# Score products of a small attention: four f32 products on all 128 rows, or twenty-four of the rounded type on 64 rows each

## The chip, the cores and the metric

The kernel runs on one core of one Trainium2 chip. Its time is the device time of one execution, in microseconds. TensorE multiplies, ScalarE and VectorE read its results from the accumulation banks and compute elementwise, SyncE (SP) and GpSimd (Pool) mostly start transfers.

## The reference, cut to what matters

A tower for 1024 samples. An encoder makes four "states" of width 512 per sample, each with a real and an imaginary part (`sr`, `si`). The stage of this case is the attention over the four states of one sample, with 8 heads of width 64:

```python
qr = heads(sr @ Wq_r.T + bq_r); qi = heads(si @ Wq_i.T + bq_i)   # k, v alike
ar = einsum('bhnd,bhmd->bhnm', qr, kr) + einsum('bhnd,bhmd->bhnm', qi, ki)
ai = einsum('bhnd,bhmd->bhnm', qi, kr) - einsum('bhnd,bhmd->bhnm', qr, ki)
w = softmax(sqrt(ar**2 + ai**2 + 1e-8) * HD**-0.5)
out_r = einsum('bhnm,bhmd->bhnd', w, vr); out_i = einsum('bhnm,bhmd->bhnd', w, vi)
attn_r = out_r @ Wo_r.T + bo_r; attn_i = out_i @ Wo_i.T + bo_i
```

Around it stand the encoders before (two large layers for each part, about the first half of the time) and, after it, a pairwise combination of the states and a small network.

## The kernel before

**Types.** The large products are done in three passes of a rounded type (`F32R`): each operand is split into a rounded part ("high") and the rest ("low"), and `split3` (lines 53 to 55) multiplies high x high, high x low and low x high into the same bank. The score products alone, with the turning and the mixing, are done on f32 operands directly.

**Blocks and steps.** `phase_states` takes 64 samples at a time: 16 blocks, each of 256 columns (`C`: 4 states x 64 samples), in two groups of 128 columns (`NG` = 2, each 32 samples with their 4 states). The width of 512 is done in 4 steps `m` of 128, that is two heads `h` of 64 each. `e` is 0 for the real and 1 for the imaginary part. Blocks 0, 1 and 15 are written out, 2 to 14 are a loop on every engine.

**TensorE's order.** In each step `m` of block `b`: `project(b, m, 0)` (Q: 24 products of 256 columns into bank `b_q`, there is only one) and `project(b, m, 1)` (K: 24 products, into one of two banks `b_k`); then, for the block before, `t_turn` (four transposes of the softmax weights, line 2014); then `score(b, m-1)` (line 2004); then `mix(b-1, m-1)` (weights times values, line 2025). After step 3 come `values(b, 0)` and `(b, 1)`, turn, score and mix of the last step, `values(b, 2)` and `(b, 3)`, and `project_out(b-1, m)` for the four `m`, 24 products each.

**Scores before.** The contraction is over both parts at once: `qs` holds, for one head, the real part of Q on partitions 0 to 63 and the imaginary part on 64 to 127. `ks` holds two arrangements of K next to each other, (real, imaginary) and (-imaginary, real), so that one product on 128 rows with 256 moving columns gives `ar` and `ai` of one head and one group. A step takes 2 heads x 2 groups = 4 such products.

**Who fills them.** ScalarE's `q_evac` adds the bias and copies Q from the bank into `qs` (4 operations on 64 partitions, line 1287). VectorE's `k_evac` makes the two arrangements of K (8 operations on 64 partitions, line 1590). `q_read` and `k_read` then free the banks and let `score` start. In the same step ScalarE also copies the turned weights (`pt_evac`, 1302), squares the scores (`t_square`, 1296) and rounds the attention's output (`o_high`, 1311, behind the mixing); VectorE spreads the weights over a mask (`spread`, 1639, behind the turns), takes the output's rest (`o_low`, 1648), and adds, masks and reduces the squared scores (`pick`, 1600 to 1609). The turns of the next step wait for `o_low`.

**Storing.** At a block's end, `t_high` (ScalarE, 1339) and `t_low` (VectorE, 1659) split the projected outputs of step `m` into slot `m % 2` of the tile `at`, and SP's `store_a` writes each step in four transfers of 128 KB. `t_high` of step `m` waits for the store of step `m - 2` (`a_stored`).

Of the kernel before, what the change touches and what calls it, by code (L numbers as in the profile page):

```python
# [14 lines left out]
P = 128  # L15
# [891 lines left out]
def phase_states(nc, g):  # L907
# [15 lines left out]
    with s.ctx:  # L923
# [8 lines left out]

        sx = sb_t("sx", [P, 2, 2, NG, KD, P], F32R)

        qs = sb_t("qs", [P, 2, 2, C])
        ks = sb_t("ks", [P, 2, 2, 2, C])
        v = sb_t("v", [P, NG, H, 2, HD])
        sq = sb_t("sq", [P, 2, W])
        m2 = sb_t("m2", [P, W])
# [1 line left out]
        ptl = sb_t("ptl", [P, 2, W])  # L941
        ohi = sb_t("ohi", [P, KD, 2, C], F32R)
        olo = sb_t("olo", [P, KD, 2, C], F32R)
        at = sb_t("at", [P, 2, 2, 2, C], F32R)
        thi, tlo = at[:, 0], at[:, 1]
        mg2 = sb_t("mg2", [P, KD, GH, N])
        tmag = sb_t("mag", [P, KD, GH, N])
        top = sb_t("top", [P, KD, GH])
# [45 lines left out]
        x_loaded = [s.sem(f"t_s_loaded{e}") for e in range(2)]  # L994
        projected = s.sem("t_projected")
        q_read = s.sem("t_q_read")
        k_read = [s.sem(f"t_k_read{h}") for h in range(2)]
        v_full = s.sem("t_v_full")
        v_read = s.sem("t_v_read")
        scored = s.sem("t_scored")  # L1000
# [82 lines left out]
        b_pm = g.ps[:, 5, :]  # L1083
        b_vo = g.ps[:, 6:8, :]
        b_val = [b_vo[:, 0, :], b_vo[:, 1, :], b_q, b_k[:, 0, :]]
        K_PARTS = ((0, 0, 0, 1), (0, 1, 1, 1), (1, 0, 1, 1), (1, 1, 0, -1))

        def half(h):
            return slice(h * HD, (h + 1) * HD)
# [166 lines left out]
        @block.gpsimd  # L1256
        def _(pool):
            def fold(t):
                pool.wait_ge(folded, t * 2 + 1)
                if not isinstance(t, int) or t < LAST:  # L1260
                    pool.wait_ge(newton, t * 2 + 3)
                pool.wait_ge(stored, t * 16)
                pool.tensor_tensor(sup[:, :, :], cs[:, :, 2, :], cs[:, :, 3, :], ALU.add).then_inc(folded, 1)

            pool.memset(k01[:, 0:1], FLOOR).then_inc(k_made, 1)
            pool.memset(k01[:, 1:2], 1.0).then_inc(k_made, 1)
            pool.wait_ge(ids_in, 16)
            for t in range(TT):
                pool.wait_ge(projected, (t + 2) * 8 + 5)
                for f, tbl in enumerate((g.tbl_0, g.tbl_1, g.tbl_2, g.tbl_3)):  # L1270
                    pool.indirect_dma_start(
                        out=emb[:, t, f * N:(f + 1) * N], out_offset=None, in_=tbl,
                        in_offset=bass.IndirectOffsetOnAxis(ap=ids[:, t, f:f + 1].bitcast(U32), axis=0)).then_inc(emb_in, 16)
            fold(0)
            with pool.Fori(1, LAST) as t:
                fold(t)
            fold(LAST)

        @block.scalar
        def _(act):  # L1280
            def q_evac(b, m):
                if not isinstance(b, int) or 4 * b + m >= 2:
                    act.wait_ge(scored, b * 8 + (2 * m - 2))
                act.wait_ge(projected, b * 8 + (2 * m + 1))
                for e in range(2):
                    for h in range(2):
                        ins = act.activation(qs[half(e), m % 2, h, :], b_q[half(h), e * C:(e + 1) * C], ACT.Identity,
                                             bias=bcol(M_Q + e, m, half(h)))
                    ins.then_inc(q_read, 1)

            def t_square(b, m):
                for h in range(2):
# [53 lines left out]

            def block_body(b, first):
                q_evac(b, 0)
                for m in range(1, KD):
                    q_evac(b, m)  # L1350
                    if not first:
                        pt_evac(b - 1, m - 1)
                    t_square(b, m - 1)
                    if not first:
                        o_high(b - 1, m - 1)
                    if first and m == 1:
                        pieces(M_V * KD, M_O * KD)
                    if first and m == 3:
                        pieces(M_O * KD, NP)
                if not first:  # L1360
                    pt_evac(b - 1, KD - 1)
                t_square(b, KD - 1)
                if not first:
                    o_high(b - 1, KD - 1)
                for i in range(4):
                    v_evac(b, i)
                t_magnitude(b)
                if not first and not last(b):
                    t_high(b - 1, 0)
                exponent(b)  # L1370
                if not first and not last(b):
                    for m in range(1, KD):
                        t_high(b - 1, m)

            blocks(act, block_body)
            block_body(LAST_B, False)

# [203 lines left out]

        @block.vector
        def _(dve):
            def k_evac(b, m):
                if not isinstance(b, int) or 4 * b + m >= 2:
                    dve.wait_ge(scored, b * 8 + (2 * m - 2))
                dve.wait_ge(projected, b * 8 + (2 * m + 2))
                for h in range(2):
                    for e, part, at_half, sign in K_PARTS:
                        ins = dve.tensor_scalar(ks[half(at_half), m % 2, h, part, :], b_k[half(h), m % 2, e * C:(e + 1) * C],  # L1590
                                                bcol(M_K + e, m, half(h)), float(sign), ALU.add, ALU.mult)
                    ins.then_inc(k_read[h], 1)

            def pick(b, m):

# [73 lines left out]
                                      ALU.subtract).then_inc(w_split, 1)  # L1669

            def block_body(b, first):
                k_evac(b, 0)
                for m in range(1, KD):
                    if not first:
                        spread(b - 1, m)
                    k_evac(b, m)
                    if not first:
                        o_low(b - 1, m - 1)
                    pick(b, m - 1)
                    if first and m == 1:  # L1680
                        pieces(M_V * KD, M_O * KD)
                    if first and m == 3:
                        pieces(M_O * KD, NP)
                pick(b, KD - 1)
                if not first:
                    o_low(b - 1, KD - 1)
                shift(b)
                if not first and not last(b):
                    t_low(b - 1, 0)
                total(b)  # L1690
                spread(b, 0)
                if not first and not last(b):
                    for m in range(1, KD):
                        t_low(b - 1, m)
# [259 lines left out]
        def _(pe):  # L1954
            def project(b, m, i):

                pe.wait_ge(w_split, (M_Q, M_K)[i] * KD + 2 * KD)
                if i == 0:
                    if not isinstance(b, int) or 4 * b + m >= 1:
                        pe.wait_ge(q_read, b * 8 + 2 * m)  # L1960
                elif not isinstance(b, int) or 4 * b + m >= 2:
                    for h in range(2):
                        pe.wait_ge(k_read[h], b * 4 + (m - 1))
                if m == 0 and not (isinstance(b, int) and b == 0):
                    pe.wait_ge(v_read, b * 4 - (1 - i))
                out = b_q if i == 0 else b_k[:, m % 2, :]
                for e in range(2):
                    pe.wait_ge(x_loaded[e], b * 32 + 32)
                    for k in range(KD):
                        w = ((M_Q, M_K)[i] + e) * KD + k  # L1970
                        mm = split3(pe.matmul, out[:, e * C:(e + 1) * C], whi[:, w, m * P:(m + 1) * P],
                                    wlo[:, w, m * P:(m + 1) * P], sx[:, e, 0, :, k, :], sx[:, e, 1, :, k, :],
                                    k == 0, k == KD - 1)
                mm.then_inc(projected, 1)

            def values(b, i):
                pe.wait_ge(w_split, M_O * KD)
                e, gr = i // 2, i % 2
                if i == 2:
                    pe.wait_ge(q_read, b * 8 + 8)  # L1980
                elif i == 3:
                    for h in range(2):
                        pe.wait_ge(k_read[h], b * 4 + 3)
                elif not isinstance(b, int) or b >= 2:
                    pe.wait_ge(t_split, b * 8 - (10 - 2 * i))
                elif b == 1:
# [5 lines left out]
                mm.then_inc(v_full, 1)  # L1992

            def score(b, m):
                pe.wait_ge(q_read, b * 8 + (2 * m + 2))
                for h in range(2):
                    pe.wait_ge(k_read[h], b * 4 + (m + 1))
                for h in range(2):
                    if not isinstance(b, int) or 4 * b + m >= 1:
                        pe.wait_ge(t_squared, b * 8 + (2 * m - 1 + h))  # L2000
                    for gr in range(NG):
                        cols = slice(gr * P, (gr + 1) * P)
                        out = b_sc[:, h, :].rearrange("p (a g c) -> p a g c", a=2, g=NG)[:, :, gr]
                        mm = pe.matmul(out, qs[:, m % 2, h, cols], ks[:, m % 2, h, :, cols], start=True, stop=True)
                    mm.then_inc(scored, 1)

            def t_turn(b, m):
                pe.wait_ge(pd_made, b * 4 + (m + 1))
# [219 lines left out]
def build(nc, g):  # L2228
    with ExitStack() as ctx:
# [10 lines left out]
        g.ids_sb = s.sb("ids", [P, TT, N], mybir.dt.int32)  # L2240
        g.emb = s.sb("emb", [P, TT, N * N])
        g.k01 = s.sb("k01", [P, 2])
        s.align(512)
        with ExitStack() as first:
            g.x_all = first.enter_context(nc.sbuf_tensor("x_all", [P, KI, TOK], F32))
# [102 lines left out]
```

## Time and profile before

| what | value |
|---|---|
| median of 3 runs | 2947.16 us (2946.24 to 2949.06) |
| the profiled execution | 2950.54 us |
| its span, first to last instruction | 2948.7 us |
| mean granted clock of TensorE | 0.979 |
| TensorE busy | 2815.6 us, 95% |
| VectorE busy | 2105.5 us, 71% |
| ScalarE busy | 1326.6 us, 45% |

The stage of the change lies from about 1424 to 2410 us; the first score product starts at 1437.7 us, the last at 2320.7 us. Records of TensorE overlap: each lasts longer than the distance to the next one's start, since products are pipelined. The distance between starts is what one costs in a dense stretch.

### The profile page before, as it was taken

The page shows a single profiled execution, that of the slowest core. Times are in us where ns is not written, and L with a number is a line of the kernel's source. Part 1 is how long each engine was busy: PE and PEld are TensorE (multiplying, and loading weights), DVE is VectorE, ACT ScalarE, POOL GpSimd, SP SyncE. Part 2 cuts the span into 40 slices and gives each one's busy share as a digit, 9 for nine tenths or more (in the row PEclk, how much of TensorE's full clock was granted, in tenths as well). Part 3 has the DMA queues.
Part 4 walks back from the last instruction along what each step waited for, and adds up shares of the span by engine and source line. Part 5 has one row for each costly group of instructions (what it writes and reads, how often), then busy time and mean ns, then how long its engine had stood idle before and what let it go on. Part 6 is the DMA issues. An engine that isn't in the chain of part 4 may idle for free. (4 is left out here: it accounts for less than half of the span.)

```text
span 2948.7 us, 40983 instructions
## 1 busy us (share of the span) xinstructions
PE 2815.6 (95%) x15040; PEld 2438.5 (83%) x15040; DVE 2105.5 (71%) x3170; ACT 1326.6 (45%) x2000; POOL 139.8 (5%) x177
## 2 busy tenths in 40 slices
PE   8999999998999989999699999999999899999797
PEld 6888888886788877888599999999999877777686
DVE  5788768763668856787667667766776759999863
ACT  2222432243534344333455555555555654555553
POOL 1000100001001010000001001000000000000000
PEclk9999999998999999999899999999999999999899
DMA  6565465545738776486422232233223464344310
GB/s 241 188 208 187 170 225 189 187 138 179 244 113 263 251 254 202 142 266 242 172 58 58 79 92 57 59 91 78 57 71 94 105 163 103 93 101 123 111 40 11
DMA packets 493712, 420.36 MB, mean 143 GB/s; under 512 B 282272, under 2 KB 397088, under 8 KB 493344
## 3 DMA queue, kind: packets, MB, share of 16 engines
q1 hardware_dynamic: 459168, 341.20, 38.2%
q0 software_dynamic: 17792, 60.89, 5.4%
q10 hardware_dynamic: 16640, 16.78, 1.7%
q8 instruction: 70, 1.15, 0.2%
q14 instruction: 42, 0.34, 0.0%
HBM read 328.62 MB, written 90.18 MB: 142 GB/s over the span
## 5 line engine op out<-in xcount | busy, mean ns | idle before, releaser
L53 PE MATMUL banks<-a_hi 128*128 128x512 f32 x1024 | 399.6, 390 | 14.3 <-DVE a_lo L353 14.3
L54 PE MATMUL banks<-a_lo,a_hi 128*128 128x512 f32 x1024 | 399.3, 390 | 0.0
L55 PE MATMUL banks<-a_hi,a_lo 128*128 128x512 f32 x1024 | 399.3, 390 | 0.0
L53 PE MATMUL banks<-b_hi 128*128 128x512 f32 x896 | 357.0, 398 | 24.3 <-DVE b_lo L760 14.0
L55 PE MATMUL banks<-b_hi,b_lo 128*128 128x512 f32 x896 | 352.5, 393 | 0.0
L54 PE MATMUL banks<-b_lo,b_hi 128*128 128x512 f32 x896 | 352.4, 393 | 0.0
L53 PE MATMUL banks<-t_sx,g_hi 128*128 128x256 f32 x1024 | 294.6, 288 | 26.5 <-DMA t_sx<-s_scr 26.5
L54 PE MATMUL banks<-t_sx,g_hi 128*128 128x256 f32 x1024 | 291.5, 285 | 0.0
L55 PE MATMUL banks<-t_sx,g_lo 128*128 128x256 f32 x1024 | 291.5, 285 | 0.0
L1590 DVE TENSOR_SCALAR t_ks<-banks,cols 64x256 f32<-64x256 f32 x512 | 236.5, 482 | 75.2 <-PE banks L55 67.9
L53 PEld LDWEIGHTS banks<-a_hi 128*128 128x128 f32 x1024 | 192.9, 188 | 54.6 <-DVE a_lo L353 14.7
L55 PEld LDWEIGHTS banks<-a_hi,a_lo 128*128 128x128 f32 x1024 | 192.8, 188 | 40.2
L54 PEld LDWEIGHTS banks<-a_lo,a_hi 128*128 128x128 f32 x1024 | 192.8, 188 | 40.0
L53 PEld LDWEIGHTS banks<-b_hi 128*128 128x128 f32 x896 | 170.4, 190 | 66.0 <-DVE b_lo L760 28.8
L53 PE MATMUL banks<-g_hi,s_axng 128*128 128x512 f32 x512 | 203.6, 398 | 18.2 <-DVE s_cs L1732 14.6
L53 PEld LDWEIGHTS banks<-t_sx,g_hi 128*128 128x128 f32 x1024 | 198.4, 194 | 27.2 <-issue 23.1
L54 PE MATMUL banks<-g_lo,s_axng 128*128 128x512 f32 x512 | 202.5, 395 | 0.0
L55 PE MATMUL banks<-g_hi,s_axng 128*128 128x512 f32 x512 | 202.3, 395 | 0.0
L55 PEld LDWEIGHTS banks<-b_hi,b_lo 128*128 128x128 f32 x896 | 170.4, 190 | 36.4
L54 PEld LDWEIGHTS banks<-b_lo,b_hi 128*128 128x128 f32 x896 | 170.8, 191 | 34.3
L54 PEld LDWEIGHTS banks<-t_sx,g_hi 128*128 128x128 f32 x1024 | 198.5, 194 | 0.1
L55 PEld LDWEIGHTS banks<-t_sx,g_lo 128*128 128x128 f32 x1024 | 198.3, 194 | 0.0
(192 smaller groups left out, 5828.9 us busy)
## 6 DMA issues: line engine op xcount, KB each, us to landing
w_ring<-w_first SPq DMA_DIRECT2D x192, 512.0 KB, 4.3
w_ring<-w_second SPq DMA_DIRECT2D x160, 512.0 KB, 5.0
t_sx<-s_scr SPq DMA_DIRECT2D x64, 512.0 KB, 4.3
a_scr<-t_at SPq DMA_DIRECT2D x256, 128.0 KB, 1.9
s_axng<-a_scr SPq DMA_DIRECT2D x64, 512.0 KB, 5.4
g_wraw<-w_pieces SPq DMA_DIRECT2D x74, 256.0 KB, 4.7
x_raw<-h_scr ACTq DMA_DIRECT2D x16, 1024.0 KB, 7.0
w_ring<-w_second SPq DMA_DIRECT2D x64, 256.0 KB, 5.0
```

Of the source, the lines that this page charges most:

```text
L53: mm(out, ahi, bhi, start=first, stop=False, **more)
L54: mm(out, ahi, blo, start=False, stop=False, **more)
L55: return mm(out, alo, bhi, start=False, stop=last, **more)
L1590: ins = dve.tensor_scalar(ks[half(at_half), m % 2, h, part, :], b_k[half(h), m % 2, e * C:(e + 1) * C], bcol(M_K + e, m, half(h)), float(s ...
```

## The change

Each score is now computed like the other large products, in three passes of high and low parts. `q_evac` makes the high part of Q for both heads at once (2 operations on 128 partitions) and a new `k_evac` on ScalarE the high part of K in three pieces: imaginary, real, minus imaginary (3 operations). VectorE's new `q_rest` and `k_rest` make the low parts (2 and 3 operations on 128 partitions) and free the banks. A head's 64 values of one part stand on 64 partitions, so a product contracts over 64 rows of the array: head 0 on the lower half, head 1 on the upper. Real and imaginary are two products that are added in the bank, times three passes: six products for each head and group, 24 in a step. For a group they are issued as six of head 0 and then six of head 1.

Two more things go with it. The tile `at` is dropped, and `thi`, `tlo` (what is stored) are now the high and low part of `qs`; so `q_evac` of steps 0 and 1 waits for the stores of the block before (`a_stored`). And `score` waits once for both heads' squares (`t_squared`) instead of once per head. The Pool queue computes the negated K bias `nbk` once at the stage's start.

```diff
@@ -932,8 +932,7 @@
 
         sx = sb_t("sx", [P, 2, 2, NG, KD, P], F32R)
 
-        qs = sb_t("qs", [P, 2, 2, C])
-        ks = sb_t("ks", [P, 2, 2, 2, C])
+        ks = sb_t("ks", [P, 2, 2, 3, C], F32R)
         v = sb_t("v", [P, NG, H, 2, HD])
         sq = sb_t("sq", [P, 2, W])
         m2 = sb_t("m2", [P, W])
@@ -941,8 +940,8 @@
         ptl = sb_t("ptl", [P, 2, W])
         ohi = sb_t("ohi", [P, KD, 2, C], F32R)
         olo = sb_t("olo", [P, KD, 2, C], F32R)
-        at = sb_t("at", [P, 2, 2, 2, C], F32R)
-        thi, tlo = at[:, 0], at[:, 1]
+        qs = sb_t("qs", [P, 2, 2, 2, C], F32R)
+        thi, tlo = qs[:, 0], qs[:, 1]
         mg2 = sb_t("mg2", [P, KD, GH, N])
         tmag = sb_t("mag", [P, KD, GH, N])
         top = sb_t("top", [P, KD, GH])
@@ -994,7 +993,9 @@
         x_loaded = [s.sem(f"t_s_loaded{e}") for e in range(2)]
         projected = s.sem("t_projected")
         q_read = s.sem("t_q_read")
-        k_read = [s.sem(f"t_k_read{h}") for h in range(2)]
+        k_read = s.sem("t_k_read")
+        q_high = s.sem("t_q_high")
+        k_high = s.sem("t_k_high")
         v_full = s.sem("t_v_full")
         v_read = s.sem("t_v_read")
         scored = s.sem("t_scored")
@@ -1083,7 +1084,6 @@
         b_pm = g.ps[:, 5, :]
         b_vo = g.ps[:, 6:8, :]
         b_val = [b_vo[:, 0, :], b_vo[:, 1, :], b_q, b_k[:, 0, :]]
-        K_PARTS = ((0, 0, 0, 1), (0, 1, 1, 1), (1, 0, 1, 1), (1, 1, 0, -1))
 
         def half(h):
             return slice(h * HD, (h + 1) * HD)
@@ -1264,6 +1264,8 @@
 
             pool.memset(k01[:, 0:1], FLOOR).then_inc(k_made, 1)
             pool.memset(k01[:, 1:2], 1.0).then_inc(k_made, 1)
+            pool.tensor_scalar(g.nbk[:, :], g.cols[:, COL_BC + (M_K + 1) * KD:COL_BC + (M_K + 2) * KD], -1.0, None,
+                               ALU.mult).then_inc(k_made, 1)
             pool.wait_ge(ids_in, 16)
             for t in range(TT):
                 pool.wait_ge(projected, (t + 2) * 8 + 5)
@@ -1281,12 +1283,20 @@
             def q_evac(b, m):
                 if not isinstance(b, int) or 4 * b + m >= 2:
                     act.wait_ge(scored, b * 8 + (2 * m - 2))
+                if m < 2 and (not isinstance(b, int) or b >= 2):
+                    act.wait_ge(a_stored[m], b * 128 - 64)
                 act.wait_ge(projected, b * 8 + (2 * m + 1))
                 for e in range(2):
-                    for h in range(2):
-                        ins = act.activation(qs[half(e), m % 2, h, :], b_q[half(h), e * C:(e + 1) * C], ACT.Identity,
-                                             bias=bcol(M_Q + e, m, half(h)))
-                    ins.then_inc(q_read, 1)
+                    ins = act.activation(qs[:, 0, m % 2, e, :], b_q[:, e * C:(e + 1) * C], ACT.Identity, bias=bcol(M_Q + e, m))
+                ins.then_inc(q_high, 1)
+
+            def k_evac(b, m):
+                act.wait_ge(projected, b * 8 + (2 * m + 2))
+                bank = b_k[:, m % 2, :]
+                act.activation(ks[:, 0, m % 2, 0, :], bank[:, C:2 * C], ACT.Identity, bias=bcol(M_K + 1, m))
+                act.activation(ks[:, 0, m % 2, 1, :], bank[:, 0:C], ACT.Identity, bias=bcol(M_K, m))
+                act.activation(ks[:, 0, m % 2, 2, :], bank[:, C:2 * C], ACT.Identity, scale=-1.0,
+                               bias=g.nbk[:, m:m + 1]).then_inc(k_high, 1)
 
             def t_square(b, m):
                 for h in range(2):
@@ -1346,10 +1356,12 @@
 
             def block_body(b, first):
                 q_evac(b, 0)
+                k_evac(b, 0)
                 for m in range(1, KD):
                     q_evac(b, m)
                     if not first:
                         pt_evac(b - 1, m - 1)
+                    k_evac(b, m)
                     t_square(b, m - 1)
                     if not first:
                         o_high(b - 1, m - 1)
@@ -1372,6 +1384,7 @@
                     for m in range(1, KD):
                         t_high(b - 1, m)
 
+            act.wait_ge(k_made, 3)
             blocks(act, block_body)
             block_body(LAST_B, False)
 
@@ -1581,15 +1594,22 @@
 
         @block.vector
         def _(dve):
-            def k_evac(b, m):
-                if not isinstance(b, int) or 4 * b + m >= 2:
-                    dve.wait_ge(scored, b * 8 + (2 * m - 2))
-                dve.wait_ge(projected, b * 8 + (2 * m + 2))
-                for h in range(2):
-                    for e, part, at_half, sign in K_PARTS:
-                        ins = dve.tensor_scalar(ks[half(at_half), m % 2, h, part, :], b_k[half(h), m % 2, e * C:(e + 1) * C],
-                                                bcol(M_K + e, m, half(h)), float(sign), ALU.add, ALU.mult)
-                    ins.then_inc(k_read[h], 1)
+            def q_rest(b, m):
+                dve.wait_ge(q_high, b * 4 + (m + 1))
+                for e in range(2):
+                    ins = dve.scalar_tensor_tensor(out=qs[:, 1, m % 2, e, :], in0=b_q[:, e * C:(e + 1) * C],
+                                                   scalar=bcol(M_Q + e, m), in1=f32(qs[:, 0, m % 2, e, :]),
+                                                   op0=ALU.add, op1=ALU.subtract)
+                ins.then_inc(q_read, 1)
+
+            def k_rest(b, m):
+                dve.wait_ge(k_high, b * 4 + (m + 1))
+                bank = b_k[:, m % 2, :]
+                for part, e in ((0, 1), (1, 0), (2, 1)):
+                    ins = dve.scalar_tensor_tensor(out=ks[:, 1, m % 2, part, :], in0=bank[:, e * C:(e + 1) * C],
+                                                   scalar=bcol(M_K + e, m), in1=f32(ks[:, 0, m % 2, part % 2, :]),
+                                                   op0=ALU.add, op1=ALU.subtract, reverse1=part == 2)
+                ins.then_inc(k_read, 1)
 
             def pick(b, m):
 
@@ -1669,11 +1689,13 @@
                                       ALU.subtract).then_inc(w_split, 1)
 
             def block_body(b, first):
-                k_evac(b, 0)
+                q_rest(b, 0)
+                k_rest(b, 0)
                 for m in range(1, KD):
                     if not first:
                         spread(b - 1, m)
-                    k_evac(b, m)
+                    q_rest(b, m)
+                    k_rest(b, m)
                     if not first:
                         o_low(b - 1, m - 1)
                     pick(b, m - 1)
@@ -1957,10 +1979,9 @@
                 pe.wait_ge(w_split, (M_Q, M_K)[i] * KD + 2 * KD)
                 if i == 0:
                     if not isinstance(b, int) or 4 * b + m >= 1:
-                        pe.wait_ge(q_read, b * 8 + 2 * m)
+                        pe.wait_ge(q_read, b * 4 + m)
                 elif not isinstance(b, int) or 4 * b + m >= 2:
-                    for h in range(2):
-                        pe.wait_ge(k_read[h], b * 4 + (m - 1))
+                    pe.wait_ge(k_read, b * 4 + (m - 1))
                 if m == 0 and not (isinstance(b, int) and b == 0):
                     pe.wait_ge(v_read, b * 4 - (1 - i))
                 out = b_q if i == 0 else b_k[:, m % 2, :]
@@ -1977,10 +1998,9 @@
                 pe.wait_ge(w_split, M_O * KD)
                 e, gr = i // 2, i % 2
                 if i == 2:
-                    pe.wait_ge(q_read, b * 8 + 8)
+                    pe.wait_ge(q_read, b * 4 + 4)
                 elif i == 3:
-                    for h in range(2):
-                        pe.wait_ge(k_read[h], b * 4 + 3)
+                    pe.wait_ge(k_read, b * 4 + 3)
                 elif not isinstance(b, int) or b >= 2:
                     pe.wait_ge(t_split, b * 8 - (10 - 2 * i))
                 elif b == 1:
@@ -1992,17 +2012,21 @@
                 mm.then_inc(v_full, 1)
 
             def score(b, m):
-                pe.wait_ge(q_read, b * 8 + (2 * m + 2))
-                for h in range(2):
-                    pe.wait_ge(k_read[h], b * 4 + (m + 1))
-                for h in range(2):
-                    if not isinstance(b, int) or 4 * b + m >= 1:
-                        pe.wait_ge(t_squared, b * 8 + (2 * m - 1 + h))
-                    for gr in range(NG):
-                        cols = slice(gr * P, (gr + 1) * P)
-                        out = b_sc[:, h, :].rearrange("p (a g c) -> p a g c", a=2, g=NG)[:, :, gr]
-                        mm = pe.matmul(out, qs[:, m % 2, h, cols], ks[:, m % 2, h, :, cols], start=True, stop=True)
-                    mm.then_inc(scored, 1)
+                pe.wait_ge(q_read, b * 4 + (m + 1))
+                pe.wait_ge(k_read, b * 4 + (m + 1))
+                if not isinstance(b, int) or 4 * b + m >= 1:
+                    pe.wait_ge(t_squared, b * 8 + 2 * m)
+                q, k = qs[:, :, m % 2], ks[:, :, m % 2]
+                passes = [(e, x, y) for e in range(2) for x, y in ((0, 0), (0, 1), (1, 0))]
+                for gr in range(NG):
+                    cols = slice(gr * P, (gr + 1) * P)
+                    for h in range(2):
+                        for i, (e, x, y) in enumerate(passes):
+                            bank = b_sc[:, h, :].rearrange("p (a g c) -> p a g c", a=2, g=NG)[:, :, gr]
+                            mm = pe.matmul(bank, q[half(h), x, e, cols], k[half(h), y, 1 - e:3 - e, cols],
+                                           start=i == 0, stop=i == len(passes) - 1)
+                            if gr == NG - 1 and i == len(passes) - 1:
+                                mm.then_inc(scored, 1)
 
             def t_turn(b, m):
                 pe.wait_ge(pd_made, b * 4 + (m + 1))
@@ -2240,6 +2264,7 @@
         g.ids_sb = s.sb("ids", [P, TT, N], mybir.dt.int32)
         g.emb = s.sb("emb", [P, TT, N * N])
         g.k01 = s.sb("k01", [P, 2])
+        g.nbk = s.sb("nbk", [P, KD])
         s.align(512)
         with ExitStack() as first:
             g.x_all = first.enter_context(nc.sbuf_tensor("x_all", [P, KI, TOK], F32))
```

## Rows read from the trace of the kernel before

**Rows 1.** The page's first part: busy time, share of the span, instructions of each engine.

```profile
PE 2815.6 (95%) x15040; PEld 2438.5 (83%) x15040; DVE 2105.5 (71%) x3170; ACT 1326.6 (45%) x2000; POOL 139.8 (5%) x177
```

**Rows 2.** Busy time by stretch: length, PE, PEld, DVE, ACT, POOL, clock, DMA share, GB/s.

```profile
1500.00:1600.00 100.00, 100.00 (x716) 94.79 (x716) 66.47 (x159) 51.87 (x101) 3.89 (x4) 1.00 0.32 85
1600.00:1700.00 100.00, 100.00 (x705) 94.35 (x704) 74.59 (x175) 56.37 (x108) 7.71 (x8) 1.00 0.24 67
...
2200.00:2300.00 100.00, 100.00 (x725) 95.14 (x724) 65.98 (x160) 51.91 (x101) 0.00 (x0) 1.00 0.30 84
```

**Rows 3.** All waits of TensorE, 1437 to 2330 us: total, times, longest.

```profile
PE banks L53 <- DMA t_sx<-s_scr: 3.8, 1, 3.8
```

**Rows 4.** Timeline of TensorE, one step: start us, length us, records.

```profile
1830.66 0.60 PE L2014 MATMUL banks<-ident,t_pd 128*128 128x128 f32 x4
1831.10 1.89 PE L2004 MATMUL banks<-t_ks,t_qs 128*128 128x256 f32 x8
1832.82 1.05 PE L2025 MATMUL banks<-t_ptl,t_v 128*128 128x128 f32 x8
1833.63 0.36 PE L53 MATMUL banks<-t_sx,g_hi 128*128 128x256 f32 x1
```

**Rows 5.** Groups by line, scores: busy us, mean ns of one record | idle before.

```profile
L2004 PE MATMUL banks<-t_ks,t_qs 128*128 128x256 f32 x512 | 121.2, 379 | 0.0
...
L2004 PEld LDWEIGHTS banks<-t_ks,t_qs 128*128 128x128 f32 x512 | 92.4, 190 | 10.1
```

**Rows 6.** Timeline of TensorE: first product of a block's first, of its third projection.

```profile
1876.88 0.28 PE L53 MATMUL banks<-t_sx,g_hi 128*128 128x256 f32 x1
...
1882.64 0.28 PE L53 MATMUL banks<-t_sx,g_hi 128*128 128x256 f32 x1
```

**Rows 7.** Groups by line, evacuations of VectorE and ScalarE.

```profile
L1590 DVE TENSOR_SCALAR t_ks<-banks,cols 64x256 f32<-64x256 f32 x512 | 236.5, 482 | 75.2 <-PE banks L55 67.9
...
L1648 DVE SCALAR_TENSOR_TENSOR t_olo<-banks,cols,t_ohi 64x256 fp32r<-64x256 f32 x256 | 123.6, 483 | 12.2 <-ACT t_ohi L1311 5.4
...
L1287 ACT ACTIVATE t_qs<-banks,cols 64x256 f32<-64x256 f32 x256 | 120.3, 470 | 140.3 <-PE banks L55 137.1
...
L1339 ACT ACTIVATE t_at<-banks,cols 128x256 fp32r<-128x256 f32 x128 | 53.7, 471 | 90.3 <-DMA a_scr<-t_at 70.3 <-PE banks L55 20.0
```

**Rows 8.** Timeline of ScalarE in the step of rows 4.

```profile
1831.37 0.60 ACT L1302 ACTIVATE t_ptl<-banks 128x512 f32<-128x512 f32 x1 [1.46 <-PE banks L2014]
...
1833.91 1.93 ACT L1311 ACTIVATE t_ohi<-banks,cols 64x256 fp32r<-64x256 f32 x4 [0.29 <-PE banks L2025]
```

**Rows 9.** Timeline of VectorE in the step of rows 4.

```profile
1831.30 1.14 DVE L1639 SCALAR_TENSOR_TENSOR t_pd<-t_ex,t_inv,mask 128x128 f32<-128x128 f32 x4 [2.41 <-PE banks L2014]
1832.47 3.78 DVE L1590 TENSOR_SCALAR t_ks<-banks,cols 64x256 f32<-64x256 f32 x8
1836.29 2.00 DVE L1648 SCALAR_TENSOR_TENSOR t_olo<-banks,cols,t_ohi 64x256 fp32r<-64x256 f32 x4
...
1840.37 1.13 DVE L1639 SCALAR_TENSOR_TENSOR t_pd<-t_ex,t_inv,mask 128x128 f32<-128x128 f32 x4
```

**Rows 10.** Timeline of VectorE at a block's end: low parts of steps 0 and 2.

```profile
1869.47 1.13 DVE L1659 SCALAR_TENSOR_TENSOR t_at<-banks,cols,t_at 128x128 fp32r<-128x128 f32 x4 [1.13 <-ACT t_at L1339]
...
1875.32 1.13 DVE L1659 SCALAR_TENSOR_TENSOR t_at<-banks,cols,t_at 128x128 fp32r<-128x128 f32 x4 [1.63 <-ACT t_at L1339]
```

**Rows 11.** Timeline of ScalarE there: high part of step 2, first Q copies.

```profile
1874.38 0.84 ACT L1339 ACTIVATE t_at<-banks,cols 128x256 fp32r<-128x256 f32 x2 [2.22 <-DMA a_scr<-t_at]
...
1879.96 1.93 ACT L1287 ACTIVATE t_qs<-banks,cols 64x256 f32<-64x256 f32 x4 [1.60 <-PE banks L55]
```

**Rows 12.** Timeline at the stage's start: Pool's second memset, ScalarE's first Q copies.

```profile
1417.91 0.10 POOL L1266 MEMSET g_k<- 128x1 f32 x1
...
1429.18 1.93 ACT L1287 ACTIVATE t_qs<-banks,cols 64x256 f32<-64x256 f32 x4 [18.32 <-PE banks L55]
```

## The prediction

> **What bounds the kernel now.** I read the page's busy shares first. TensorE is busy 95% of the span, and the next engine, VectorE, 71% [rows 1]. A busy share is an average, so the table by stretches came next, over the stage that the change touches (from about 1437 to 2330 us). From 1500 us TensorE is busy for every microsecond, at a granted clock of 1.00, while VectorE has 66 to 75 in a hundred and ScalarE 52 to 56 [rows 2]. Third, the list of TensorE's waits over that stage holds a single one, of 3.8 us, for a load in block 1 [rows 3]. So here TensorE's instruction stream is the time. What the other engines do is free until it makes TensorE wait, and what is added to TensorE is added to the span.
>
> A busy TensorE says nothing about what one instruction costs, because each record lasts longer than the distance to the next. I therefore took distances between starts from the timeline. In one step the four turns start at 1830.66, the scores at 1831.10, the mixing at 1832.82, the next projection at 1833.63 [rows 4]. The scores thus hold TensorE for 1.72 us. Rows 5 show 512 score records for 16 blocks x 4 steps x 4 products = 256 products: each f32 product is recorded as two. A step has eight records, 0.215 us apart, and the score records last 379 ns [rows 5]. For the rounded type (F32R), a projection product also streams 256 columns; 48 of them lie between 1876.88 and 1882.64 [rows 6], which is 0.120 us each.
>
> **The change on TensorE.** It removes 4 products a step (1.72 us) and adds 2 groups x 2 heads x 6 = 24, each 256 columns of the rounded type, on 64 rows. No product of this kernel uses fewer than 128 rows, so the price of one is not in the trace and has to be bounded.
> - Nearest row: the same columns and type on 128 rows, 0.120 us. 24 x 0.120 = 2.88 us, so a step grows by 1.16 us. There are 16 x 4 = 64 steps: +74.2 us. Halving the rows shortens neither the columns streamed (256) nor the columns loaded as weights (128), so I give no discount for it. I take this value.
> - Below: products on different halves of the array could run at once. In this order that is possible only where one head's sixth product meets the other head's first, three times in a step. Three slots less are 21 x 0.120 = 2.52 us, +0.80 x 64 = +51 us.
> - Weight loads speak against much of that. Each product has its own. In the four turns, load and product together are 0.44 / 4 = 0.11 us apart [rows 4], the closest spacing of loads that I use; 24 such loads take 2.64 us, +0.92 x 64 = +59 us, whatever the products do.
> - Above: going from whole-array to half-array products and back could empty the array twice a step. A record of 0.28 us [rows 6] at a distance of 0.120 has 0.16 us of tail; two are 0.32 us, +20.5 us over 64 steps, in all +95 us.
>
> The Trainium skill states this last as a rule (TensorEngine Tiling (Array Packing), Key Properties): a change of tiling mode drains TensorE. By the rule the sum would be the +95 us just worked out, without it +74; no record here shows it.
>
> The additions into the bank (six products into one place) are priced at nothing extra, since the projection's twelve products per output are added up in the same way at 0.120 us.
>
> **The evacuations.** Per step ScalarE gives up 4 Q copies on 64 partitions (470 ns each) and does 2 for Q and 3 for K on 128 partitions (also 470, by the t_at row) [rows 7]: +0.47 us, about 30 us over the stage. VectorE gives up 8 K copies of 482 ns and does 5 rests; the nearest row is the t_olo rest, 483 ns [rows 7]: 3.86 becomes 2.42 us, 92 us less in the stage. Neither counts in itself, both have idle time. What counts is order. Q and K become ready only after both engines, one behind the other.
>
> I follow a step from T = 1831.3, when the turns are done. ScalarE copies the turned weights until T+0.7 [rows 8], then the three K parts until T+2.1. VectorE spreads until T+1.2 [rows 9], finishes the Q rest at T+2.2 and the K rest at T+3.6. The bank of Q is needed by the next projection after scores and mixing, at T-0.2+2.88+0.81 = T+3.5: 1.3 us to spare. K has two banks and is used a whole step later. Behind that, the high part of the outputs starts when mixing is done (T+3.8) and takes 1.93 [rows 8], the low part 2.00 [rows 9], together until T+7.8. The next turns need it at T-0.2+2.88+0.81+2x2.88 = T+9.2. VectorE's last three operations of 0.7 end at T+9.9, and the next turns are done at about T+9.9. Before, a step was 0.44 + 1.72 + 0.81 + 5.76 = 8.7 us on TensorE and 1840.37 - 1831.30 = 9.1 on VectorE [rows 9], which made it up at the block's end; now both have 9.9, so the step stays covered. If the cover were gone, each 0.1 us would cost 64 x 0.1 = 6.4 us.
>
> **The shared tile.** Now the stored result's tile is Q's tile, so at a block's start the Q copy also waits until the store of two steps before has landed. ScalarE's own wait shows how long that takes. The low part of step 0 runs from 1869.47 to 1870.60 [rows 10], and the high part of step 2 starts at 1874.38 behind its store [rows 11], 3.8 us later. For the next block the relevant low part ends at 1876.45 [rows 10], landing about 1880.2. The Q copy starts at 1879.96 now [rows 11] and would start at 1880.2. With 0.95 for two copies and 1.1 for two rests and the handover it is done at 1882.3, against a need at 1882.64 [rows 6]. That leaves 0.3 us, every block. Behind the waiting copy on ScalarE stand the K copies of step 0, whose data come 2.9 us later anyway. In the first two blocks with this pattern the store may come later; I add 0.5 us for both. VectorE's rest for Q is behind nothing else there, and the SP queue issues the same stores in the same order. If the margin were gone, and the store 0.3 us later than it has to be, 14 blocks would lose 4 us.
>
> **The rest.** The scores' one wait for both heads' squares asks for squares that were finished some 5 us before, so it costs nothing. The Pool queue's new small operation follows two memsets of 0.1 us at 1417.9, and ScalarE's first copy is at 1429.18 [rows 12]: 11 us of cover, price nothing. In block 0 the weight pieces sit ahead of the Q rest of step 2 on VectorE; longer scores push its need later by more than the rest takes, so nothing. The 3.8 us wait for the load stays, since its order isn't touched. DMA traffic is the same.
>
> **The sum.** 64 x 1.16 = 74.2, plus 0.5, is 74.7 us. The profiled execution took 2950.54 us (span 2948.7 and 1.8 around it), and so becomes 3025.2. It lies 3.4 us above the median of the runs, so the forecast is 3022 us, 2.5% more.
>
> **Rivals.**
> - Overlap at the three changes of head: 2947 + 51 = 2998 us, or 3006 if loads stay 0.11 us apart. For it: the halves are independent and write different banks. Against: only one load's spacing fits between two products. Chance 0.20. The Trainium skill (TensorE: Matmul & The Clock Gate, Part 3) has products on different row groups run together but start and end in program order, which would give exactly these three meetings and no more.
> - Emptying at both borders: 2947 + 95 = 3042 us. Against: going from turns to scores and from mixing to projection, other changes of kind, leaves no such gap [rows 4]. Chance 0.17.
> - The two heads really side by side, six against six, at twelve slots: 1.44 us a step, 0.28 less than now, -18 us, 2929 us. That is the other side. It is one mechanism, and it decides when a product costs less than 1.72 / 24 = 0.072 us. Against: it needs products of the second head to pass five of the first, and loads every 0.06 us, where 0.11 is the least seen. Chance 0.08.
> - Loads that aren't hidden in half-array products: 0.120 + 0.190 (the load's record, [rows 5]) = 0.31 a product, 7.44 a step, +366 us, 3313 us. Against: whole-array products hide them. Chance 0.05.
> - The three passes gain as much as they cost, within 0.2% (about what a measurement of this kernel can tell from no change): a product at 0.07 us. Chance 0.02.
>
> The forecast itself has 0.48. Faster is the side-by-side case, 0.08; the same 0.02; slower 0.90. The range takes in overlap (2998) and emptying (3042), with some microseconds beyond each for the handovers of Q and the store: 2990 to 3050, which leaves out the side-by-side and the unhidden-load cases and a little more.
>
> **What would show it.** In the changed profile: 1536 score records (from 512) at starts 0.12 us apart; from the first score to the first mixing 2.9 us instead of 1.72; no wait of TensorE for the Q or K rests; a block 4.6 us longer than now; VectorE's time down by some 90 us, ScalarE's up by 30. Two products of different heads starting together would mean overlap; a longer distance at the first score and the first mixing, emptying. The prediction fails if the distance between scores isn't 0.12, or if TensorE waits at the second projection of a block.

## The result: 1.0% slower, where 2.5% was forecast

The changed kernel takes 2977.4 us in the median (2974.33 to 2981.45), the kernel before 2946.7 us: ratio 1.0101, 95% interval 1.0086 to 1.0115. The profiled execution took 2977.36 us, with a span of 2975.6 us. That is 31 us more in the medians (27 between the two profiled executions), outside my range of 2990 to 3050, though on the forecast side. In the traces the stretch from the first to the last score product grew from 883.0 to 912.2 us, by 29.2; the time behind it was 2 us shorter.

The page's first part of the changed kernel, against [rows 1]:

```profile
PE 2843.8 (96%) x16064; PEld 2460.7 (83%) x16064; DVE 2002.8 (67%) x2978; ACT 1322.4 (44%) x2064; POOL 142.5 (5%) x178
```

VectorE has 103 us less, and ScalarE, which got a whole new job, 4 us less. A stretch of the stage, same columns as [rows 2], still has TensorE busy all the time at full clock:

```profile
1700.00:1800.00 100.00, 100.00 (x825) 95.85 (x824) 54.27 (x142) 51.05 (x107) 8.27 (x8) 1.00 0.28 74
```

TensorE's waits from 1437 to 2420 us, so with the stage's tail, which [rows 3] leave out:

```profile
PE banks L2038 <- DVE t_pd L1659: 6.3, 1, 6.3
PE banks L53 <- DMA t_sx<-s_scr: 3.9, 1, 3.9
PE banks L53 <- DVE t_olo L1668: 3.1, 1, 3.1
PE banks L53 <- DVE t_qs L1679: 0.9, 2, 0.5
PE banks L53 <- issue: 0.7, 1, 0.7
```

The first, second and fourth were there before, within 0.1 us (turns of the last block, the load of block 1, the last low parts), the third was 2.3 us. The fifth is new. It stands once, in block 0, ahead of the Q projection of step 3. In the first row here, from the load engine's list over the same time, its wait is put down to VectorE's weight pieces (L1688); in the next two the Q rest of step 2 stands behind these pieces, and TensorE goes on when it is done:

```profile
PEld banks L53 <- DVE g_lo L1688: 0.9, 1, 0.9
...
1442.20 4.90 DVE L1688 TENSOR_TENSOR g_lo<-g_wraw,g_hi 128x512 fp32r<-128x512 f32 x8
1447.02 0.87 DVE L1600 SCALAR_TENSOR_TENSOR t_qs<-banks,cols,t_qs 128x256 fp32r<-128x256 f32 x2
...
1447.99 0.35 PE L53 MATMUL banks<-t_sx,g_hi 128*128 128x256 f32 x1 [0.74 <-issue]
```

Apart from these 0.7 us the time went into TensorE's own stream. One step of it, the counterpart of [rows 4]:

```profile
1803.02 0.60 PE L2038 MATMUL banks<-ident,t_pd 128*128 128x128 f32 x4
1803.55 2.04 PE L2026 MATMUL banks<-t_ks,t_qs 64*128 64x256 f32 x24
1805.51 1.16 PE L2049 MATMUL banks<-t_ptl,t_v 128*128 128x128 f32 x8
1806.43 0.48 PE L53 MATMUL banks<-g_hi,t_sx 128*128 128x512 f32 x1
```

From the first turn to the next projection or value product it is 3.41 us; in [rows 4] it was 2.97. The 0.44 us, 64 times, are 28 of the 29 us. All 24 products start within 1.76 us, so they cannot be 0.12 us apart one behind the other. The same view cut off after a few products shows why. The first row ends the window at 1803.892, the second 6 ns later:

```profile
1803.55 0.62 PE L2026 MATMUL banks<-t_ks,t_qs 64*128 64x256 f32 x3
...
1803.55 0.73 PE L2026 MATMUL banks<-t_ks,t_qs 64*128 64x256 f32 x4
```

The third product of head 0 and a fourth record start within some nanoseconds, and the fourth is a long one (it ends at 1804.28), like the first product of a stream. From there starts come in pairs. These rows carry no head, but the starts sort into two rows of twelve, each 0.12 us apart, the second 0.35 us behind the first. The last product of each head raises the semaphore `scored`, and the two records of the trace that do so start 0.35 us apart, at 1804.957 and 1805.305. The two heads run side by side.

This gives a sum of a step that I then tested: 12 slots of 0.12 instead of 1.72 us, 0.28 less; 0.35 more because the second head starts late; and 0.38 at the borders, where turns to first score, first to second score, last score to mixing and first to second mixing product take about 0.09 to 0.10 us more each than the spacing inside those groups. In all +0.45 us.

### The profile page after: what moved, and what is told of

It is laid out like the page before. It is cut to its first block and busy times, and to the rows that moved or that the text cites. A ratio compares the mean times of both kernels' runs of the same rounds, so it can differ in the third digit from the quotient of the medians.

```text
span 2975.6 us, 42798 instructions
## 1 busy us (share of the span) xinstructions
PE 2843.8 (96%) x16064; PEld 2460.7 (83%) x16064; DVE 2002.8 (67%) x2978; ACT 1322.4 (44%) x2064; POOL 142.5 (5%) x178
## 5 line engine op out<-in xcount | busy, mean ns | idle before, releaser
L1668 DVE SCALAR_TENSOR_TENSOR t_olo<-banks,cols,t_ohi 64x256 fp32r<-64x256 f32 x256 | 123.6, 483 | 92.3 <-ACT t_ohi L1321 87.2
```

Source lines behind the costliest of these rows:

```text
L1668: ins = dve.scalar_tensor_tensor(out=olo[half(h), m, e, :], in0=pm(b, m)[half(e), h * C:(h + 1) * C], scalar=bcol(M_V + e, m, half(h)), in ...
```

## The experiments

All start from the changed kernel. Edits are cut to the lines that matter. Times are medians, ratios against the kernel before, run on the same chip as the experiment (not always the same one), and "a step" is the stretch from the first turn to the next product behind the mixing (the median of 58 steps of the profile from 1500 us on).

**Alternating.** Only the order of the products changes, in short:

```diff
-for gr in range(NG): for h in range(2): for i in range(6)
+for gr in range(NG): for i in range(6): for h in range(2)
```

> The 24 score products of a step are issued alternately, one of head 0 and one of head 1; nothing else changes. In the changed kernel the second head's stream starts 0.35 us after the first one's, and both then run side by side, 12 products each at 0.12 us. Theory D (each half of the array has its own queue, the issue in program order gets at most some three products ahead in a half): the second stream starts at once, a step from the turns to the next projection falls from 3.41 to 3.06 us, 64 x 0.35 = 22 us less, about 2955 us. Theory R (the issue takes 0.029 us an instruction, 12 instructions before the second head's first, and has no limit ahead): the start comes 0.06 us late, 3.12 us, 19 us less, about 2959 us. If the heads in fact run one behind the other with meetings only where the head changes: 23 meetings, no such sum as above; the step would be the same as with D.

Measured: 2957.41 us, ratio 1.0028 (1.0018 to 1.0038). A step takes 3.06 us. In this row the window ends some 10 ns after the first start, and two products are under way:

```profile
1796.66 0.39 PE L2025 MATMUL banks<-t_ks,t_qs 64*128 64x256 f32 x2
```

The 0.35 us were the late start and nothing else. Order alone is worth 20 us.

**Twelve and twelve.**

```diff
-for gr in range(NG): for h in range(2): for i in range(6)
+for h in range(2): for gr in range(NG): for i in range(6)
```

> All 12 products of head 0 are issued, then all 12 of head 1. Theory D (a queue for each half, the issue some three products ahead): the second stream starts when nine products of the first are through, 9 x 0.12 = 1.08 us instead of 0.35; a step 4.13 us, 46 us more than the changed kernel, about 3023 us. Theory R (0.029 us an instruction, no limit ahead): start after 24 x 0.029 = 0.70 us, a step 3.76 us, 22 us more, about 3000 us. Only a meeting at the one change of head, as in my prediction: 23 slots, 0.5 us more than now by 1 slot less than D, 3031 us.

Measured: 3018.65 us, 1.0232 (1.0213 to 1.0251); a step 4.12 us. Windows that end at 1811.135 and 1811.145:

```profile
1810.08 1.33 PE L2025 MATMUL banks<-t_ks,t_qs 64*128 64x256 f32 x9
...
1810.08 1.44 PE L2025 MATMUL banks<-t_ks,t_qs 64*128 64x256 f32 x10
```

Nine start, then the second head's first, 1.06 us after the start and right behind the ninth. That is the start that theory D gives; R's 0.70 us and 3000 us are out, and so is the single meeting of my prediction with 3031 us.

**Runs of three and of four.** The order within a step is written as runs of 3, and of 4 (which cross from group 0 to group 1).

```diff
+[(gr, h, 3 * j + i) for gr in range(NG) for j in range(2) for h in range(2) for i in range(3)]
...
+[(n // 6, h, n % 6) for j in range(3) for h in range(2) for n in range(4 * j, 4 * j + 4)]
```

> Runs of three products of a head. Theory D: three fit into the first head's queue, so the second starts within about 0.1 us; a step 3.1 us, 20 us less than the changed kernel, about 2957 us. Theory R: 6 instructions ahead of the second head, 0.17 us, a step 3.23 us, 11 us less, about 2966 us.

Measured: 2956.0 us, 1.0023 (1.0013 to 1.0033); a step 3.07 us. D, not R.

> Runs of four products of a head. In the measured orders the second head's first product started just behind the running start of the first head's third (runs of six) and ninth (runs of twelve), and at once with runs of three: that is, always with three products of the first head still to start. If that is the rule, four behave as three: the first is running, three are waiting, the second head starts within about 0.02 us, a step 3.07 us, about 2956 us. If only three in all can be handed over, running one included, the second head starts with the first head's second, 0.22 us late, a step 3.29 us, about 2970 us.

Measured: 2965.09 us, 1.0051 (1.0034 to 1.0068); a step 3.17 us. The second head does start at once, 0.013 us after the first (the window ends 20 ns after the first start):

```profile
1838.97 0.39 PE L2025 MATMUL banks<-t_ks,t_qs 64*128 64x256 f32 x2
```

But the step is 0.10 us longer than I expected. In the records the second head's fifth product, first of its second run, starts in its turn, is as long as a stream's first (0.380 us), and the sixth comes 0.22 us behind it instead of 0.12: the same extra 0.10 us as at a border. The load engine shows why. Inside a stream the load of a product starts right behind the start of the product before it, 0.12 us ahead of its own. Windows of the load engine that end at 1839.552 and 1839.560:

```profile
1839.43 0.30 PEld L2025 LDWEIGHTS banks<-t_ks,t_qs 64*128 64x128 f32 x2
...
1839.43 0.30 PEld L2025 LDWEIGHTS banks<-t_ks,t_qs 64*128 64x128 f32 x3
```

The load that the second row has more is that of the second head's fifth product. It starts at 1839.553, 0.11 us behind the start of the head's fourth product, 5 ns behind the start of the first head's fifth (1839.548) and 6 ns ahead of its own. So this product was handed over only when three of the first head's were left to start, too late to be loaded ahead. No run changes this by itself.

What these orders don't show is a queue for each half. One count of four products handed over and not yet started, whichever half they are for, explains them as well: worked through with 0.22 us for a stream's first product and 0.12 for the others, both rules give the same start of the second head in all five orders.

**Whole array, twelve and twenty-four.** The half is dropped from both operands (so the heads are added up), with all 24 products or, in the other run, with 12: one group's six for each of the two banks.

```diff
-pe.matmul(bank, q[half(h), x, e, cols], k[half(h), y, 1 - e:3 - e, cols], ...)
+pe.matmul(bank, q[:, x, e, cols], k[:, y, 1 - e:3 - e, cols], ...)
```

> The score products take all 128 rows and there are 12 in a step, six for each bank (the two heads are added up and one group of each bank is left out, so the scores are not the reference's). The evacuations are those of the changed kernel. If the gaps at both ends of the scores (0.09 and 0.10 us before the second product, 0.09 and 0.10 before the second mixing product, in all 0.38) come from going to half-array products and back, they vanish: a step 0.44 + 1.44 + 0.81 = 2.69 us, 46 us less than the changed kernel, about 2931 us. If they come from the change of type or of source, they stay: 3.07 us, about 2955 us.

Measured: 2933.8 us, 0.9946 (0.9929 to 0.9964); a step 2.68 us:

```profile
1793.54 0.60 PE L2036 MATMUL banks<-ident,t_pd 128*128 128x128 f32 x4
1793.89 1.67 PE L2025 MATMUL banks<-t_ks,t_qs 128*128 128x256 f32 x12
1795.40 1.05 PE L2047 MATMUL banks<-t_ptl,t_v 128*128 128x128 f32 x8
```

The step is as long as 0.44 + 1.44 + 0.81 us, turns, twelve slots and mixing, with no time lost at either end. (The rows have 0.35 and 1.51 for the first two: the first score starts some 0.08 us early and the second as much later.) The alternating kernel has the same twelve slots, the same type and neighbours, and 0.38 us more. So the gaps belong to the change between whole-array and half-array products. The load engine has them too. The first of these rows is its list of waits in the changed kernel, 1437 to 2420 us; no whole-array kernel has such a row for its scores. The second is its timeline at the step shown above:

```profile
PEld banks L2026 <- issue: 10.4, 61, 0.4
...
1803.54 0.53 PEld L2026 LDWEIGHTS banks<-t_ks,t_qs 64*128 64x128 f32 x5 [0.17 <-issue]
```

The first load stands still for 0.17 us and then starts with its product (1803.55) and not 0.12 us ahead, which goes with the 0.10 us before a stream's second product.

> All 24 score products of a step, but each on 128 rows (the two heads are added up, so the scores are not the reference's); evacuations and order as in the changed kernel. This is the price of my prediction, 0.120 us a product without any running side by side: a step 0.44 + 2.88 + 0.81 = 4.13 us, 46 us more than the changed kernel, about 3023 us. If half-array products are slower or faster in themselves than whole ones, this run and that of twelve in a row differ by it.

Measured: 3022.51 us, 1.0245 (1.0228 to 1.0262); a step 4.12 us. My forecast was 3022: its price was that of this kernel. That twelve and twelve has the same step is an accident: its 21 slots and the 0.38 us of borders make 2.90 us, 24 slots 2.88.

**Evacuations alone.** Four f32 products on 128 rows in place of the 24:

```diff
+mm = pe.matmul(bank, f32(q[:, 0, h, cols]), f32(k[:, 0, 1 - h:3 - h, cols]), start=True, stop=True)
```

> The changed kernel's evacuations, shared tile and waits, with the score products of the kernel before in number, type and rows: four f32 products on 128 rows (on the high parts of one part each, so the scores are not the reference's). My prediction has this part at 0.5 us: 2947 to 2948 us. The rival, that the longer way of Q and the shared tile make TensorE wait at each block's second projection, would give 4 us or more, 2951 us, with waits of TensorE for the Q rest in the list.

Measured: 2952.03 us against 2950.38 of the kernel before on that chip, 1.0004 (0.9995 to 1.0014), a step 2.975 us as before. The interval, 1.5 us less to 4.1 more, doesn't quite exclude the rival's 4 us; the list of TensorE's waits does, for it has none that comes back in every block. It has the one of block 0 again, and the first to the last score product take 884.7 us against 883.0:

```profile
PE banks L53 <- DVE g_lo L1688: 1.1, 1, 1.1
```

The longer way of Q, the new job of ScalarE and the shared tile cost about 1.7 us in the stage of this one trace, and nothing that the medians can tell from zero.

**Two visits.** Group 0's products stand before the turns, in the alternating order:

```diff
-t_turn(b - 1, m - 1)
-score(b, m - 1)
+score(b, m - 1, (0,))
+t_turn(b - 1, m - 1)
+score(b, m - 1, (1,))
```

> The alternating order, but group 0's products stand before the turns and group 1's behind them, so that TensorE goes to half-array products and back twice in a step. If each such visit costs 0.38 us at its two ends whatever is in it, a step (from the first score to the next projection) grows from 0.53 less, 3.06 in all, to 3.44 us: 64 x 0.38 = 24 us more than the alternating order, about 2981 us. If the gaps belong to the particular neighbours (turns, mixing) and not to the change of array use, the new neighbour, a projection, shows none: about 12 us more, 2969 us.

Measured: 2989.14 us, 1.0136 (1.0119 to 1.0153), spans 2986.7 against 2955.4: 31 us more than alternating, where I expected 24.

```profile
1807.07 0.28 PE L55 MATMUL banks<-t_sx,g_lo 128*128 128x256 f32 x1
1807.28 0.98 PE L2026 MATMUL banks<-t_ks,t_qs 64*128 64x256 f32 x12
1808.19 0.66 PE L2038 MATMUL banks<-ident,t_pd 128*128 128x128 f32 x4
1808.77 0.98 PE L2026 MATMUL banks<-t_ks,t_qs 64*128 64x256 f32 x12
1809.68 1.16 PE L2049 MATMUL banks<-t_ptl,t_v 128*128 128x128 f32 x8
1810.59 0.48 PE L53 MATMUL banks<-g_hi,t_sx 128*128 128x512 f32 x1
```

From the last projection product before to the next one behind it is 3.52 us here; in the alternating order it is 3.06 and the normal 0.12 before the turns, 3.18. So a second visit costs 0.34 us, 20 us over the 60 steps that have turns between the groups, and a projection as neighbour is no exception (0.21 us before the first score). The rest is a wait that this order brings in. In two of a block's four steps the next projection starts later and the step is 0.28 and 0.41 us longer, which makes 10 us in 15 blocks. One of these steps, and the list of waits from 1500 to 2300 us, which books 7 of the 10:

```profile
1860.13 1.16 PE L2049 MATMUL banks<-t_ptl,t_v 128*128 128x128 f32 x8
1861.43 0.39 PE L53 MATMUL banks<-t_sx,g_hi 128*128 128x256 f32 x1
...
PEld banks L53 <- DVE t_qs L1600: 7.1, 26, 0.3
```

From mixing to projection it is 1.30 us there, and 0.91 in the step above. The Q rest stands on VectorE behind the spreading, and so behind the turns. With the turns 1.0 us later the next Q projection catches up with it.

## Why the prediction missed

**The bound** was right: TensorE's stream is the time, at full clock. One term that I had put at nothing costs 0.7 us, the Q rest behind the weight pieces in block 0. It followed from the price: I had the longer scores push the need for it back by 1.16 us, but they did so by 0.44. The run of 24 whole-array products, which has my price, has no such wait.

**The price of a product** failed. The term was 24 x 0.120 = 2.88 us one behind the other, +1.16 us a step; measured, a step grew by 0.44. I had the number of a slot right (0.12 us in each stream) and its count wrong: two heads in step would fill 12, and six against six fill 12 and a late start of three, 15. The overlap rival was wrong as well, in that it let the heads meet only where the runs touch. Its reason was that a product starts only after all before it in the program. Measured, the order holds within a half only: in the changed kernel the second head's first product starts while three of the first head's six still wait. The Trainium skill's sentence that products start and end in program order (TensorE: Matmul & The Clock Gate, Part 3) isn't what these records show.

**The side-by-side rival**, to which I gave 0.08, has the right mechanism, and my argument against it was wrong twice. The second head's products pass only products of the other half, and of those no more than three at a time. And 0.11 us between the loads of the turns [rows 4] was no limit of the loads: in the alternating kernel 24 products, each with its load, start in 1.41 us, one in 0.06. Its time of 2929 us was wrong too, for it left out both other terms.

**Emptying at the borders**, to which I gave 0.17, was real besides: I estimated 0.32 us a step from the tails, measured 0.38 in one visit and 0.34 for a second. The trace agrees with the rule of the Trainium skill that I had quoted (TensorEngine Tiling (Array Packing), Key Properties). My argument against it, that other changes of kind leave no gap, compared whole-array products with each other. My rivals were alternatives, each with its own time. They were terms of one sum: -0.28 + 0.35 + 0.38 us, 64 times, +29 us. No rival had the late start of 0.35 us.

**The evacuations** went nearly as forecast in what counts (about 1.7 us, where I had 0.5) and kept their engines busy for less than priced. Two Q copies of ScalarE on 128 partitions take 0.84 us and three rests of VectorE 1.26:

```profile
1805.62 1.26 DVE L1609 SCALAR_TENSOR_TENSOR t_ks<-banks,cols,t_ks 128x256 fp32r<-128x256 f32 x3
...
1835.91 0.84 ACT L1290 ACTIVATE t_qs<-banks,cols 128x256 fp32r<-128x256 f32 x2 [2.00 <-DMA a_scr<-t_qs]
1838.43 0.47 ACT L1296 ACTIVATE t_ks<-banks,cols 128x256 fp32r<-128x256 f32 x1 [1.68 <-PE banks L55]
```

Such records are as long as those on 64 partitions (470 to 483 ns) but follow each other after 0.37 to 0.40 us, where four on 64 partitions took 1.93 us. ScalarE's forecast +30 us became -4, because I had added up lengths of records where, as on TensorE, the distance of starts is the price; [rows 11] had 0.84 us for two such copies already. The row of L1290 shows the shared tile: at this block's start the Q copy waits for the store, as I had worked out, and no wait of TensorE follows. The margin for Q inside a step was real too, since the two-visits kernel used it up.

## What to carry to other kernels

Products on different halves of the array are two streams. Count them per half, issue them alternately or in runs of no more than three, and add what entering and leaving half-array use costs (0.38 us a visit here): with both, twelve slots against 1.72 us of f32 products still lost 0.3%. When two rivals touch different parts of a sum, price them together and not as alternatives. The kernel before remains the fastest that computes the reference. The twelve whole-array products (0.5% faster) point to real and imaginary part stacked on 128 rows in rounded and rest parts; that needs 24 evacuations on 64 partitions a step. An estimate: at 0.49 us each (four take 1.93 or 2.00 us in [rows 8] and [rows 9]) they are 11.8 us. A step has 3.7 us of ScalarE besides (turned weights 0.60, two squares 1.20, `o_high` 1.93) and 5.2 of VectorE (spreading 1.14, `o_low` 2.00, three operations of 0.69). Together they make 20.7 us, and the two engines have 2 x 8.4 = 16.8 in a step of 8.4 us. It wouldn't fit without moving more work; I didn't build it.

## What the runs showed of the hardware

- The other half's first product starts as soon as no more than three of the first half's are left to start: with runs of 3, 4, 6 and 12 that was after 0.010, 0.013, 0.35 and 1.06 us. Whether the issue counts for each half isn't shown.
- Entering half-array use costs 0.09 us before the first product and 0.10 before the second of each half (the halves at the same time), and leaving it the same again; the first load isn't made ahead.
- A whole-array and a half-array product of 256 columns have the same spacing, 0.12 us in a stream; two streams side by side slow neither: 24 half-array products start within 1.41 us, 24 whole-array ones within 2.83.
- Copies of 256 columns out of a bank are recorded with 0.47 to 0.48 us on 64 as on 128 partitions, but follow each other after 0.48 to 0.50 us on 64 and after 0.37 to 0.40 on 128.
